# Local attention layers of an eight-stage kernel: entry waits, table timing, a second PSUM bank for the last unit, and stores inside the stage

## The chip, the cores and the metric

The kernel runs on one core of one Trainium2 chip. It is one program of about 102,000 instructions. The metric is the device time of one execution in microseconds (us). The engines are PE (TensorE, matrix multiplies; PEld its weight loads), DVE (VectorE), ACT (ScalarE), POOL (GpSimd) and SP (SyncE, which here only issues DMAs). Each runs its own instruction stream in order, and they meet at semaphores.

## The reference, cut to what matters

Eight blocks in a row work on 8 batches of 256 tokens with 128 channels. Each block's result is normalised and added to the residual. The change touches only the last one, six layers of local attention with a feed-forward part:

```python
x = x + _layernorm(_L3_ffn_ref(_layernorm(x), ...))

for i in range(DEPTH):
    x = attn_layer(shift_tokens(x), Wqkv[i], q_scale[i], k_scale[i], Wo[i]) + x
    x = ffn_layer(shift_tokens(x), ln_g[i], ln_b[i], W1[i], b1[i], W2[i], b2[i]) + x
# attn_layer: q, k, v of 16 heads of 64; l2-normalised; rotated by tables that hold
# cos, sin, a decay and the layer's q_scale / k_scale; softmax over windows of 32 + 32 keys; Wo
# ffn_layer: layernorm, W1, a * gelu(gate), W2
```

## The kernel before, in words

The order of all work is written out by hand. `build` runs the eight stages one after the other. Ahead of a stage `normalise_x` makes `M.xn`, the normalised tokens (16 tiles of 128 tokens, in 4 groups; DVE makes groups 0 and 2 at L495, ACT groups 1 and 3 at L489). Behind it `mark_end` drains the engines, and `add_up` normalises the stage's result `M.y` and adds it to the residual `M.x`: moments, a reciprocal square root by DVE alone (L414 to L425), the scaling (L489, L495), and per group the sum (L519) and the statistics for the next stage (L522). After the last stage SP stores `M.x` in 4 DMAs.

The last stage is `stage_local`. A **unit** is one batch in one layer: 6 x 8 = 48 units, `UNITS`. All engines loop over the same list of **steps** `s`, with `n, p = divmod(s, 8)`: a unit has 8 steps, one for each pair of heads, and a step holds work of several units at once:

- raw rows: PE multiplies a quarter row block of q or k (`a = s + 15` or `s + 16`, L3182), DVE rotates it with the tables (`dve_rope`, L3331 to L3334), POOL adds the halves (L3479, `rope_sum`), ACT squares (L3278), DVE sums the squares (L3438);
- roots of the lengths, twice a unit (`root_of`: DVE L3355, ACT L3259 and L3261, DVE L3361 to L3365);
- POOL scales the rows (L3492, `normed`), PE turns them (L406);
- scores (L3152), softmax, values (L3167), and the output projection `wo` (L3128, in steps `p` 3 and 4 of the next unit);
- two units behind: the feed-forward part (`center`, `moment`, `ones`, `gates`, `third`, `linear`, `out`). Its products, those of v and the projection share one PSUM bank, `room = Bench(M, (1,))`: `fills(s)` says which fill stands in which step, early or late, and each fill waits until the one before it was read.

The rotation tables of a layer are four POOL instructions (L3471). POOL makes them at `a = s + 15`, in the step in which DVE first needs them (`p` is 1 there). The wait in `dve_rope` is on the signal `tables`.

On entry PE turns the four groups of `M.xn` (L406 into banks 0 to 3), and signals `tile_turned`. POOL then zeroes seven places (`cleared`, L3457) and casts two constants. DVE (L3372) and ACT (L3270) copy the turned groups to `X` only once POOL has cleared all places, and PE waits for all copies, all clears and the constants before its first step.

At the end, when the last unit has been fed (L3404, L3405), DVE copies `X` (L3445, L3446), PE turns it back (16 times L406), ACT copies it to `M.y` (L3321), and `add_up` follows.

## Time and profile before

| | us |
|---|---|
| median of 3 runs | 3864.39 (3860.45 to 3868.89) |
| the profiled execution's own time | 3863.01 |
| its span in the profile | 3861.7 |
| PE busy over the span | 3142.8 (81%) |
| DVE, ACT, POOL busy | 2700.2, 2240.3, 1456.3 |
| granted clock of PE, mean | 0.929 of full |

The profile's page gives each engine's busy time, a strip of the span in 40 slices, and the chain of work that ended last. The last stage begins at about 1903 us of the span and takes the rest, half of the kernel. Its slices read 9 (90% busy or more) for PE nearly everywhere. The first of the last stage's boundaries between layers lies in the window from 2181 us, an ordinary unit in that from 3614 us. The views used below are the timeline (each row an instruction or several alike in a row: start, duration, engine, line, output and input, count, and in brackets how long the engine stood idle before it and what ended that), the busy time in chosen windows, and the answer for one source line.

### The profile page before, as it was taken

Reading aid. Unit: us, or ns where it says so; the run is one execution under the profiler, and the core shown is the slowest. Engines: PE = TensorE matmul, PEld = TensorE weight load, DVE = VectorE, ACT = ScalarE, POOL = GpSimd, SP = SyncE. Lnnn points to the kernel's source line nnn. Section 1 sums busy time; section 2 is a strip of 40 time slices with the busy share of each in tenths; the row PEclk is TensorE's granted clock in tenths of the full one; section 3 lists DMA queues with packets and bytes.
Section 4 is the critical chain, followed back from the end, with each engine's and each line's share of the span. In section 5 each row is a group of like instructions: output and inputs, shape, how many; then the busy total and the mean of one; then the engine's idle time right before and its main releaser. Section 6 shows DMA issues by size and latency. Waiting matters only on the chain.

```text
span 3861.7 us, 102257 instructions
## 1 busy us (share of the span) xinstructions
PE 3142.8 (81%) x41309; PEld 2040.7 (53%) x41309; DVE 2700.2 (70%) x7080; ACT 2240.3 (58%) x5612; POOL 1456.3 (38%) x1443
## 2 busy tenths in 40 slices
PE   6877865727776879777589999999999999999996
PEld 4544544612323546445346666666666666666664
DVE  6466666637895554589687777777777777777763
ACT  4234442426653332268557777777777777777773
POOL 0110011336671000000166556566656655656550
PEclk9989987968997989889899999999999999999996
DMA  1000002710000000000001011102010201110110
GB/s 54 1 5 1 1 12 58 221 62 0 1 0 5 2 1 1 30 1 1 30 21 31 22 31 50 31 22 60 22 31 22 60 22 31 50 31 22 31 24 19
DMA packets 50437, 108.05 MB, mean 28 GB/s; under 512 B 7360, under 2 KB 17472, under 8 KB 48176
## 3 DMA queue, kind: packets, MB, share of 16 engines
q1 hardware_dynamic: 47440, 96.33, 9.1%
q0 software_dynamic: 2528, 5.18, 0.7%
q8 instruction: 328, 5.37, 0.6%
q14 instruction: 141, 1.16, 0.1%
HBM read 52.27 MB, written 5.18 MB: 15 GB/s over the span
## 4 chain that ended last, share of the span: by engine, by line
PE 45%; DVE 23%; ACT 13%; issue 5%; POOL 3%; DMA 1%; POOLq 0%; SPq 0%; DVEq 0%; ACTq 0%
PE psum L3182 5%; PE psum L3128 5%; PE psum L401 5%; PE psum L3167 4%; PE psum L406 4%; PE psum L3088 4%; PE psum L1145 4%; PE psum L1998 3%; DVE scratch L3331 3%; PE psum L1199 2%; DVE xnT L3438 2%; DVE xnT L3363 2%; PE psum L3152 1%; DVE scratch L3333 1%; ACT weights L1388 1%
## 5 line engine op out<-in xcount | busy, mean ns | idle before, releaser
L3479 POOL TENSOR_TENSOR scratch<-scratch 128x512 f32<-128x512 f32 x384 | 488.7, 1273 | 434.9 <-DVE scratch L3334 434.9
L406 PEld LDWEIGHTS psum<-table,scratch 128*128 128x128 f32 (+1 forms) x2284 | 283.3, 145 | 297.3 <-issue 237.2
L3182 PE MATMUL psum<-weights,scratch 128*128 128x512 f32 x768 | 418.7, 628 | 18.7 <-ACT y L3278 11.5
L406 PE MATMUL psum<-table,scratch 128*128 128x128 f32 (+1 forms) x2284 | 369.8, 283 | 46.3 <-DVE scratch L2699 11.8
L3492 POOL TENSOR_TENSOR scratch<-scratch,xnT 128x512 f32<-128x512 f32 x384 | 401.6, 1046 | 0.0
L3331 DVE TENSOR_TENSOR scratch<-psum,xnT 128x512 f32<-128x512 f32 x384 | 264.6, 689 | 173.8 <-PE psum L3182 153.6
L3311 ACT COPY scratch<-psum 128x512 f32<-128x512 f32 x384 | 225.7, 588 | 163.8 <-PE psum L406 158.0
L3278 ACT ACTIVATE y<-psum 128x512 f32<-128x512 f32 x384 | 230.8, 601 | 120.6 <-DVE scratch L3334 108.0
L3438 DVE TENSOR_REDUCE xnT<-y 128x8 f32<-128x512 f32 x384 | 254.0, 661 | 1.4
L1145 PE MATMUL psum<-scratch 32*128 32x256 f32 (+1 forms) x2560 | 179.1, 392 | 69.3 <-DVE weights L1406 20.5
L3413 DVE TENSOR_REDUCE scratch<-psum 128x4 f32<-128x256 f32 x384 | 161.4, 420 | 73.8 <-PE psum L3152 72.3
L3088 PE MATMUL psum<-weights,scratch 128*64 128x512 f32 x768 | 207.1, 618 | 1.2 <-ACT scratch L3226 1.2
L3250 ACT ACTIVATE scratch<-psum,scratch 128x64 f32<-128x64 f32 x768 | 178.1, 316 | 46.8 <-DVE scratch L3413 42.7
L3182 PEld LDWEIGHTS psum<-weights,scratch 128*128 128x128 f32 x768 | 136.0, 194 | 126.6 <-issue 78.6
L3485 POOL TENSOR_TENSOR y<-scratch 128x256 f32<-128x256 f32 x192 | 117.9, 614 | 206.3 <-DVE scratch L3421 206.3
L3250 ACT ACTIVATE y<-psum,scratch 128x64 f32<-128x64 f32 x768 | 179.1, 324 | 2.8
L3152 PE MATMUL psum<-scratch 64*32 64x64 f32 x12288 | 175.4, 223 | 0.0
L1145 PEld LDWEIGHTS psum<-scratch 32*128 32x128 f32 x2560 | 119.1, 192 | 106.2 <-DVE weights L1406 32.0
L406 PE MATMUL psum<-table,xn 128*128 128x128 f32 x112 | 25.1, 415 | 183.3 <-DVE xn L495 183.3
L406 PE MATMUL psum<-table,y 128*128 128x128 f32 x784 | 152.5, 279 | 22.6 <-DVE y L495 20.8
L3167 PE MATMUL psum<-xn,scratch 64*64 64x32 f32 x6144 | 129.6, 222 | 47.5 <-ACT scratch L3311 33.0
L3485 POOL TENSOR_TENSOR y<-y,scratch 128x256 f32<-128x256 f32 x192 | 117.9, 614 | 128.0 <-DVE scratch L3421 127.7
(527 smaller groups left out, 7741.3 us busy)
## 6 DMA issues: line engine op xcount, KB each, us to landing
scratch<-scratch SPq DMA_DIRECT2D x96, 256.0 KB, 3.2
scratch<-experts_dram SPq DMA_DIRECT2D x47, 384.0 KB
scratch<-scratch SPq DMA_DIRECT2D x96, 128.0 KB, 3.2
weights<-layer_dram SPq DMA_DIRECT2D x6, 1357.0 KB, 9.5
weights<-layer_dram SPq DMA_DIRECT2D x6, 1356.5 KB, 6.9
scratch<-scratch SPq DMA_DIRECT2D x96, 64.0 KB, 2.9
weights<-gqa_dram SPq DMA_DIRECT2D x2, 1738.5 KB, 8.8
results_dram<-scratch SPq DMA_DIRECT2D x11, 256.0 KB
```

The lines of the kernel that those rows point to most:

```text
L406: return self.nc.tensor.transpose(out, src, self.c("ident")[0:k, 0:k])
L1145: last = mm(bank(n)[:, col:col + size], A.head(rows, n, at, P), A.head(cols, n, by, size), start=not A.causal, stop=True, skip_group_check ...
L3088: last = mm(bank[64 * r:64 * r + 64], window(n)[:, 64 * j:64 * j + 64], weight(n, "wqkv")[:, at:at + 512], start=True, stop=True)
L3167: last = mm(SUMS[64 * h:64 * h + 64, j, QB * q:QB * q + QB], V[u % 2][64 * r:64 * r + 64, 4 * j + q, pair * LDIM:(pair + 1) * LDIM], turne ...
L3182: mm(raw_bank(a), window(m)[:, i * P:i * P + P], weight(m, "wqkv")[:, at:at + 512], start=True, stop=True).then_inc(S("rows_made").up(), 1)
L3250: last = nc.scalar.activation(E[s % 2][:, 2 * j + (h ^ j), :], scores(s)[:, h, 64 * j:64 * j + 64], ACT.Exp, bias=small[s % 4][:, 0, 2 * h ...
L3278: nc.scalar.activation(sq[a % 2], raw_bank(a), ACT.Square).then_inc(S("squared").up(), 1)
L3331: tt(heads(out), src, bc(cosine, LDIM), ALU.mult).then_inc(dve.link(), 1)
L3438: red(lengths[m % 2][:, 0, 2 + 8 * q:10 + 8 * q], heads(sq[a % 2]), AX, ALU.add).then_inc(S("lens").up(), 1)
L3479: gtt(out, out, sines, ALU.add).then_inc(S("rope_sum").up(), 1)
L3485: gtt(probs[t % 2], E[t % 2], over_keys(small[t % 4][:, 1, :]), ALU.mult).then_inc(S("divided_pool").up(), 1)
L3492: gtt(out, out, lengths[m % 2][:, 1, 2 + 8 * q:10 + 8 * q].unsqueeze(2).broadcast_to([P, HB, LDIM]), ALU.mult).then_inc(S("normed").up(), 1)
```

## The change: what it does

1. **Entry.** PE turns `M.xn` into banks 4 to 7. DVE and ACT copy without waiting for `cleared`. POOL begins once DVE has made its tiles of `M.xn`, clears one column of `X`, makes the tables of layer 0, and then clears the rest and casts. PE starts its steps at once: a unit of the first layer waits for its own columns, scores wait for the clears. ACT loads its table behind its copies.
2. **Tables.** `pool_rope(l)` makes a layer's tables at `s + 22`, seven steps sooner (in a step with `p` 2, where before it was `p` 1). DVE's wait stands.
3. **Last unit.** Unit 47 uses bank 0 for all its fills but v (`last_room`), and its steps are moved ahead by 2 (`AHEAD`; its projection by 1, all 8 pairs in one step). `unit_at` says so for each kind of work.
4. **Stores.** The last layer's batches are finished in five sets (2, 2, 2, 1 and 1 batches; `SETS`), each in the 8 steps that begin 24 steps behind its last unit's first: PE turns them back from `X` in two halves with a wait between, ACT copies, DVE takes statistics and variances; the root rides in `root_of`; ACT scales, DVE adds to `M.x`, SP stores. `mark_end` and `add_up` are not called for this stage.

```diff
-    room = Bench(M, (1,))
+    room, last_room = Bench(M, (1,)), Bench(M, (0,))
+    AHEAD = 2
+    def unit_at(s, lag, p, ahead=AHEAD):
+        last = UNITS - 1
+        if s == 8 * (last + lag) + p - ahead:
+            return last
+        n, q = divmod(s - p, 8)
+        return n - lag if q == 0 and 0 <= n - lag < last else None
+    SETS = [(UNITS - 8, 2), (UNITS - 6, 2), (UNITS - 4, 2), (UNITS - 2, 1), (UNITS - 1, 1)]
+    set_at = {f + k - 1 + 3: e for e, (f, k) in enumerate(SETS)}
...
+        if p == 0 and n in set_at:
+            early.append(("set", set_at[n], "y_out", set_at[n]))
...
         elif key == "project":
-            pe_project(n, range(4))
+            pe_project(n, range(8 if n == UNITS - 1 else 4))
...
+        elif key == "set":
+            pe.wait_ge(S("fed"), 2 * tiles_of(n)[-1][0] + 1)
+            for i, (f, j) in enumerate(tiles_of(n)):
+                last = nc.tensor.transpose(bank[:, i * P:i * P + 64], low(f)[:, j * P:j * P + P], c("ident")[0:64, 0:64])
+            last.then_inc(pe.link(), 1)
+            pe.settle()
+            for i, (f, j) in enumerate(tiles_of(n)):
+                last = nc.tensor.transpose(bank[:, i * P + 64:i * P + P], high(f)[:, j * P:j * P + P], c("ident")[64:P, 64:P])
+            last.then_inc(S("y_turned").up(), 1)
...
     def pe_program():
         M.wait_loaded(pe, "layer0")
-        pe_turn(M, M.xn)
-        pe.wait_ge(S("lowest"), GROUPS - 1)
-        pe.wait_ge(S("highest"), GROUPS - 1)
-        pe.wait_ge(S("cleared"), CLEARS - 1)
-        pe.wait_ge(S("tables"), 0)
+        for g in range(GROUPS):
+            wait_xn(M, pe, g)
+            for k in range(4):
+                last = M.flip(M.bank(4 + g)[:, P * k:P * k + P], M.xn[:, 4 * g + k, :])
+            last.then_inc(S("tile_turned").up(), 1)
...
-        dve.wait_ge(S("tables"), m // BATCH + 1)
+        dve.wait_ge(S("tables"), m // BATCH)
...
     def act_program():
...
+            if p == 5 and n in set_at:
...
+                act.wait_ge(S("y_scaled"), e)
+                for i in range(k):
+                    last = nc.scalar.activation(done[e % 2][:, i, :], done[e % 2][:, i, :], ACT.Identity, bias=r[:, 1, i:i + 1],
+                                                scale=lengths[(n + 1) % 2][:, 1, 66 + i:67 + i])
...
+    SET_WORK = {1: dve_see_set, 2: dve_set_variance, 4: dve_set_shift, 6: dve_set_add}
...
     def dve_program():
         M.wait_loaded(dve, "layer0")
-        dve.wait_ge(S("cleared"), CLEARS - 1)
...
     def pool_program():
-        M.wait_loaded(pool, "layer0")
-        pool.wait_ge(S("tile_turned"), GROUPS - 1)
...
+        pool.wait_ge(S("xn_dve"), 2 * GROUPS - 1)
+        nc.gpsimd.memset(X[64:P, :, 0:1], 0.0).then_inc(S("cleared").up(), 1)
+        pool.wait_ge(S("cleared"), 0)
+        pool_rope(0)
...
-            a = s + 15
-            if 0 <= a < PARTS and a % (8 * BATCH) == 0:
...
+            l, k = divmod(s + 22, 8 * BATCH)
+            if k == 0 and 0 < l < DEPTH:
+                pool_rope(l)
...
     def sp_program():
...
+        for e, (f, k) in enumerate(SETS):
+            tiles = slice(2 * (f % BATCH), 2 * (f % BATCH) + 2 * k)
+            sp.wait_ge(S("x_sum"), e)
+            nc.sync.dma_start(M.out[:, tiles, :], M.x[:, tiles, :]).then_inc(M.out_sem, 16)
```

`dve_see_set` takes one statistics instruction per tile, `dve_set_variance` six small instructions with two waits among them, `dve_set_shift` one, `dve_set_add` one sum over all tiles of the set.

The instruction order on POOL at the stage's entry. L3457 are the clears, L3459 and L3460 the casts, L3471 the tables, L3479 the first sums. Before:

```order
L3457 MEMSET scratch 64x8
L3457 MEMSET scratch 128x8x32 x2
L3457 MEMSET scratch 32x512 x4
L3459 CAST scratch<-table 128x128
L3460 CAST scratch<-table 128x128
L3471 TENSOR_TENSOR xnT<-table,weights 128x128 x4
L3479 TENSOR_TENSOR scratch<-scratch 128x512 x10
```

Now (L3546 and L3552 are the clears, L3540 the tables, L3566 the sums):

```order
L3546 MEMSET scratch 64x8
L3540 TENSOR_TENSOR xnT<-table,weights 128x128 x4
L3552 MEMSET scratch 128x8x32 x2
L3552 MEMSET scratch 32x512 x4
L3554 CAST scratch<-table 128x128
L3555 CAST scratch<-table 128x128
```

The tables went from behind the clears and casts to behind the first clear.

On POOL at a layer's boundary, now, the tables (L3540) stand between the row scaling of step `p` 1 (L3579) and the sum of step `p` 2 (L3566); L3572 divides the probabilities:

```order
L3566 TENSOR_TENSOR scratch<-scratch 128x512
L3572 TENSOR_TENSOR y<-scratch 128x256
L3579 TENSOR_TENSOR scratch<-scratch,xnT 128x512
L3540 TENSOR_TENSOR xnT<-table,weights 128x128 x4
L3566 TENSOR_TENSOR scratch<-scratch 128x512
L3572 TENSOR_TENSOR y<-y,scratch 128x256
```

Before, the same four stood seven rounds of these three later, ahead of the sum of the step in which the new layer's first rows are rotated.

On PE at the end of the program. L3167 are the values of the last pair of heads, L3114 and L3115 `third`, L3118 `linear`, L3128 the projection, L401 `out`, L3095 `center`, L3099 `moment`, L3104 `ones`, L3110 `gates`. Before:

```order
L3167 MATMUL psum<-xn,scratch 64x32 x16
L3114 MATMUL psum<-weights 85x256
L3115 MATMUL psum<-weights 85x256
L3118 MATMUL psum<-weights 128x256 x2
L3128 MATMUL psum<-xnT,weights 128x256 x2
L3128 MATMUL psum<-xn,weights 128x256 x6
L401 MATMUL psum<-weights 128x256 x3
L3095 MATMUL psum<-scratch,table 128x256
L3099 MATMUL psum<-table,stats 128x1 x2
L3104 MATMUL psum<-weights,table 128x128 x2
L3110 MATMUL psum<-weights 128x256 x2
```

Now (L3204 values, L3140 and L3141 `third`, L3164 projection, L3144 `linear`, L3121 `center`, L3125 `moment`, L3130 `ones`, L3136 `gates`, L3150 and L3154 the two halves of a set):

```order
L3204 MATMUL psum<-xn,scratch 64x32 x16
L3140 MATMUL psum<-weights 85x256
L3141 MATMUL psum<-weights 85x256
L3164 MATMUL psum<-xnT,weights 128x256 x2
L3164 MATMUL psum<-xn,weights 128x256 x6
L3144 MATMUL psum<-weights 128x256 x2
L3121 MATMUL psum<-scratch,table 128x256
L3125 MATMUL psum<-table,stats 128x1 x2
L401 MATMUL psum<-weights 128x256 x3
L3130 MATMUL psum<-weights,table 128x128 x2
L3136 MATMUL psum<-weights 128x256 x2
L3150 MATMUL psum<-table,scratch 128x64 x2
```

The last unit's projection went ahead of the unit before's `linear`, its `center` and `moment` ahead of that unit's `out`, and a set stands behind its `gates`. The 16 turns at the end are gone.

## Rows read from the trace of the kernel before

**Rows 1.** Windows: length, busy PE, PEld, DVE, ACT, POOL, granted clock, DMA.

```profile
2181.00:2223.90 42.90, 38.72 (x653) 26.04 (x652) 30.18 (x76) 28.84 (x82) 24.48 (x29) 0.92 0.10 24
3614.00:3652.20 38.20, 35.96 (x653) 24.35 (x653) 30.07 (x76) 28.83 (x80) 23.03 (x24) 1.00 0.12 26
```

**Rows 2.** Timeline of the stage's entry (start, duration, engine, line, what, count, idle before).

```profile
1903.45 3.19 ACT L489 ACTIVATE xn<-x,stats 128x128 f32<-128x128 f32 x8 [5.99 <-DVE stats L484]
1903.45 2.14 DVE L495 TENSOR_SCALAR xn<-x,stats 128x128 f32<-128x128 f32 x8
1904.71 3.65 PE L406 MATMUL psum<-table,xn 128*128 128x128 f32 x16 [16.62 <-DVE xn L495]
1908.50 3.15 POOL L3457 MEMSET scratch<- 64x8 f32 x7 [294.27 <-PE psum L406]
1911.74 2.48 DVE L3372 COPY scratch<-psum 64x512 f32<-64x512 f32 x4 [6.15 <-POOL scratch L3457]
1912.21 1.51 POOL L3471 TENSOR_TENSOR xnT<-table,weights 128x128 f32<-128x128 f32 x4
1915.16 5.62 PE L3182 MATMUL psum<-weights,scratch 128*128 128x512 f32 x8 [6.81 <-ACT scratch L3270]
1917.24 0.69 DVE L3331 TENSOR_TENSOR scratch<-psum,xnT 128x512 f32<-128x512 f32 x1 [3.03 <-PE psum L3182]
```

**Rows 3.** Timeline at the first and the last of five layer boundaries.

```profile
2180.21 0.66 DVE L3438 TENSOR_REDUCE xnT<-y 128x8 f32<-128x512 f32 x1
2181.95 1.51 POOL L3471 TENSOR_TENSOR xnT<-table,weights 128x128 f32<-128x128 f32 x4
2183.55 0.69 DVE L3331 TENSOR_TENSOR scratch<-psum,xnT 128x512 f32<-128x512 f32 x1 [2.68 <-issue]
...
3421.00 1.51 POOL L3471 TENSOR_TENSOR xnT<-table,weights 128x128 f32<-128x128 f32 x4
```

**Rows 4.** The answer for line L3331: its idle time over the whole span.

```profile
  issue: 13.4, 5
```

**Rows 5.** Timeline of an ordinary unit, DVE and POOL.

```profile
3650.76 1.27 POOL L3479 TENSOR_TENSOR scratch<-scratch 128x512 f32<-128x512 f32 x1 [1.35 <-DVE scratch L3334]
3650.82 1.27 DVE L3363 SCALAR_TENSOR_TENSOR xnT<-xnT 128x34 f32<-128x34 f32 x1
3655.05 0.42 DVE L3391 TENSOR_TENSOR weights<-stats,psum 128x256 f32<-128x256 f32 x1
3658.28 0.69 DVE L3331 TENSOR_TENSOR scratch<-psum,xnT 128x512 f32<-128x512 f32 x1 [1.10 <-PE psum L3182]
3659.71 1.27 POOL L3479 TENSOR_TENSOR scratch<-scratch 128x512 f32<-128x512 f32 x1 [1.41 <-DVE scratch L3334]
3664.88 1.27 POOL L3479 TENSOR_TENSOR scratch<-scratch 128x512 f32<-128x512 f32 x1 [2.33 <-DVE scratch L3334]
3693.23 0.42 DVE L3391 TENSOR_TENSOR weights<-stats,psum 128x256 f32<-128x256 f32 x1
```

**Rows 6.** Timeline of the tail, from the last values to the last statistics.

```profile
3802.59 1.08 PE L3167 MATMUL psum<-xn,scratch 64*64 64x32 f32 x32 [0.52 <-DVE xn L3383]
3806.67 2.07 PE L3118 MATMUL psum<-weights 128*128 128x256 f32 x4 [1.07 <-DVE weights L3425]
3809.71 2.08 PE L3128 MATMUL psum<-xnT,weights 128*128 128x256 f32 x4 [0.97 <-DVE weights L3396]
3824.93 0.42 DVE L3391 TENSOR_TENSOR weights<-stats,psum 128x256 f32<-128x256 f32 x1 [2.11 <-PE psum L3104]
3838.71 0.49 DVE L3405 SCALAR_TENSOR_TENSOR scratch<-psum,weights,scratch 64x256 f32<-64x256 f32 x1
3850.26 0.17 DVE L451 SCALAR_TENSOR_TENSOR stats<-stats 128x16 f32<-128x16 f32 x1
3853.06 4.73 ACT L489 ACTIVATE y<-y,stats 128x128 f32<-128x128 f32 x12 [6.93 <-DVE stats L484]
3859.36 0.87 DVE L522 BATCH_NORM_STATS2 stats<-x 128x6 f32<-128x128 f32 x4
```

More of the change, by code:

```diff
@@ L3042, in room_of, with tiles_of, room_for @@
+    def tiles_of(e):
+        f, k = SETS[e]
+        return [(f + i // 2, i % 2) for i in range(2 * k)]
+    def room_for(key, n):
+        return last_room if n == UNITS - 1 and key[0] != "v" else room
     def room_of(key, n):
-        return room.bank((key, n))
+        return room_for(key, n).bank((key, n))
     def fills(s):
         n, p = divmod(s, 8)
-        unit = lambda k: 0 <= k < UNITS
         early, late = [], []
-        if p == 0 and unit(n - 2):
-            late.append(("ones", n - 2, "scaled", n - 2))
@@ L3065, in fills @@
-        if p >= 6 and unit(n + 1):
+        if p == 0 and n in set_at:
+            early.append(("set", set_at[n], "y_out", set_at[n]))
+        for key, lag, at, when, signal, step in (
+                ("ones", 2, 0, late, "scaled", lambda f: f), ("gates", 2, 1, early, "gelu", lambda f: 3 * f + 1),
+                ("third", 2, 2, early, "gated", lambda f: 3 * f), ("linear", 2, 2, late, "gated", lambda f: 3 * f + 2),
+                ("project", 1, 3, early, "added", lambda f: 2 * f + 1), ("out", 2, 4, late, "fed", lambda f: 2 * f + 1),
+                ("center", 1, 5, early, "centered", lambda f: f), ("moment", 1, 5, late, "var_out", lambda f: f)):
+            f = unit_at(s, lag, at, 1 if key == "project" else AHEAD)
+            if f is not None:
+                when.append((key, f, signal, step(f)))
@@ L3350, in dve_clamp @@
         x = lengths[m % 2][:, 0, first:last]
+        if last > 66:
+            dve.settle()
         if m < UNITS:
```

183 lines of the change are left out of this document (107 added, 76 removed).

## The prediction

> **What bounds the kernel now.** I read the busy windows first, then the timeline at the four places that the change touches. In an ordinary unit PE is busy 35.96 of 38.20 us at the full clock, DVE 30.07, ACT 28.83 and POOL 23.03 [rows 1]. So PE sets the pace, with small gaps, and DVE and ACT have a fifth to a quarter left. The same instruction of two neighbouring units (L3391) starts at 3655.05 and 3693.23, 38.18 us apart [rows 5]: that is the rhythm of nearly all 48 units. Anything that moves the total must break this rhythm at a few places, shorten the entry or the tail, or change the rhythm itself. PE is 0.92 clocked in the boundary unit and 1.00 in the other [rows 1], which says that something stalls it there.
>
> **Entry.** PE's 16 turns end at 1904.71 + 3.65 = 1908.36. Only then does POOL clear for 3.15 us, then DVE copies, ACT copies, and the first raw rows start at 1915.16; DVE's first rotation is at 1917.24, 2.08 behind them [rows 2]. In the changed order PE goes on to the raw rows at once. Their columns are there: ACT's rows of `M.xn` end at 1903.45 + 3.19 = 1906.64 and DVE's at 1905.59 [rows 2], and group 0 can be copied by about 1907.3, while PE still turns the last group. Raw rows then start at 1908.4 instead of 1915.16: **6.8 us** sooner. What could be late next is POOL. It starts at 1905.6; 3.15 of clears, 1.51 of tables and about 0.6 of casts (estimated from the clears' size) end near 1911.0. DVE's first rotation, at 1908.4 + 2.08 = 1910.5, needs only the first clear and the tables (about 1907.4), and its sum on POOL is wanted at about 1911.9. So POOL's work is covered with 0.9 us to spare; without cover it costs at most that much again. Bounds 5.8 to 7.2.
>
> **Tables.** At a boundary DVE is done with its step at 2180.21 + 0.66 = 2180.87, PE's rows are ready, and DVE stands until POOL has made the tables (2181.95, 1.51 us): 2.68 us [rows 3]. It happens 5 times, 13.4 us in all [rows 4]. But the loss is larger. The tables of the first and the last boundary start at 2181.95 and 3421.00 [rows 3], 1239.05 us for 4 layers, that is 32 units; 32 x 38.18 = 1221.76. The rest is 17.29, or 4.32 for each boundary. The other 1.6 us is the clock: the boundary unit has 0.92 granted, so PE runs a stretch of it at the lower of its two levels (1.2 against 2.4 GHz) behind the stall, and in the ordinary unit, without a stall, it never does [rows 1]. I take it that without the stall the clock does not fall: 5 x 4.32 = 21.6. The new place costs POOL 1.51 us once a layer, in step `p` 2, where POOL stands idle for 1.41 us anyway (the gap before the sum at 3659.71) [rows 5]. That leaves about 0.1 to 0.2 us of delay, 0.5 for all five. Net **21.1 us**; bounds 12.2 (only the wait goes, each new place costs 0.24) and 21.6. The Trainium skill, page "TensorE: Matmul & The Clock Gate", Part 1, says the same of the mechanism: the lower clock is the default, idling brings it back, activity releases it. By that rule the whole 21.6 goes with the stall; by the wait alone it would be 13.4.
>
> **Sets inside the full program.** Sets 0 and 1 stand in units 44 and 46. Each adds: on PE 8 narrow turns and a wait for its own queue. 16 full turns took 3.65 at half clock, 0.23 each [rows 2]; narrow ones at full clock are at most half of that, 0.9 for 8, with the wait about 1.3. On ACT a copy (0.6) and 4 scalings of 4.73 / 12 = 0.39 [rows 6], 2.2 in all. On DVE 4 statistics (0.87 [rows 6]), six small ones and a longer clamp at 0.17 each [rows 6] with waits, about 1.1, a shift and a sum of 0.7: 2.8. What of it is on the path: PE's 1.3 fully, since PE leads there. DVE's statistics lie in step 1, ahead of a gap of 1.10 us [rows 5]: nothing. The small ones come in step 2, where the next rotation follows without a gap: 1.1. ACT's 1.6 of scalings in step 5 delay the next square, partly covered: 1.1. Together 3.5 for set 0. Set 1 is in a unit without raw rows and rotations, so only about 2.2. Sum **+5.7 us**; bounds 2.6 (PE alone, twice) and 12.6 (nothing covered: 1.3 + 2.2 + 2.8 = 6.3, twice).
>
> **One rule speaks against this part.** DVE's L3363 starts at 3650.82, 0.06 behind POOL's sum at 3650.76, and takes 1.27 us, just as long as POOL's; a DVE instruction as small took 0.17 with POOL idle [rows 5, 6]. So a small DVE instruction can wait out a whole POOL one. The new variances are such. They come at the end of step 2, though, and there POOL stands idle for 2.33 us until DVE's next rotation [rows 5], so I charge no such wait. The Trainium skill, page "SBUF — State Buffer", section "SBUF: two separate sides", describes this as an exclusive lock on a port pair that DVE and POOL share, taken by DVE instructions with two SBUF inputs. By the rule taken alone each of three waiting groups would cost a POOL instruction, some 3.5 us more a set.
>
> **Last unit.** Before, one bank forces the order third, `linear`, projection. The last values end at 3802.59 + 1.08 = 3803.67 and the last unit's L3391 starts at 3824.93 [rows 6], 21.3 us later. In it PE stands 1.07 before `linear` and 0.97 before the projection [rows 6], each time for DVE's gating, and unit 46's `out` and sum (2.5) stand ahead of the last unit's `center`. Now the projection follows `third` directly, and `out` runs while the last unit's variance goes through its root. Saved: 1.07 + 0.97 and about 1.9 of the 2.5, 3.9. Against it: set 2 (8 turns at the half clock and a copy) sits in front, +1.2. Net **2.7 us**; bounds 0 and 4.5. PE's clock decides most of that width, since it changes level here.
>
> **End.** Before, the last feed ends at 3838.71 + 0.49 = 3839.20 and the last sum at about 3859.3, where its statistics start (3859.36) [rows 6]: 20.1 us of copy, turns, moments over 16 tiles, 12 scalings, four sums. Now two tiles are left. From the feed: rest of set 3 on DVE and ACT, which covers the four turns, 1.7; copy 0.4; 2 statistics 0.43; seven small DVE steps at 0.2 (0.17 [rows 6] and a wait) 1.4; two on ACT 0.5; root 0.6; shift 0.2; two scalings 0.8; sum 0.4. That is 6.4, so 13.7 less. Set 3's turns delay `third` of the last unit by about 0.3. Net **13.4 us**; bounds 12 and 15. The stores of sets 0 to 3 lie beside other work. The last store, half as large as before, is counted as before.
>
> **Sum.** -6.8 - 21.1 + 5.7 - 2.7 - 13.4 = -38.3 us. The profiled execution took 3863.0 of its own; 3824.7 by this. The median of the runs is 1.4 above it, which gives 3826; I say 3825.
>
> **Rivals.**
> 1. The clock falls at the boundaries all the same. For it: a unit has many small gaps, and the sets add more. Against it: no ordinary unit shows it [rows 1]. Gain 38.3 - (21.1 - 12.2) = 29.4: about 3835. Chance 0.08.
> 2. The sets cost their full engine time, 12.6, and their stalls bring a stretch at the lower clock each (1.6, twice): 15.8 in place of 5.7, gain 28: about 3836. For it: L3363's 1.27 us beside POOL [rows 5], and that three engines are hit in one unit. Against it: the gaps in [rows 5]. Chance 0.14.
> 3. Sets almost free (2.6) and the tail at the full clock: gain 43: about 3821. Chance 0.08.
> 4. Slower. L3363 waits for POOL twice a unit because the two start together [rows 5]. Tables and entry shift POOL against DVE; if the rhythm settled where one more small DVE instruction a unit waits 1.27 us, 45 units would cost 57 and the time would be about 3882. It decides from 38.3 / 45 = 0.85 us a unit. Against it: after each boundary, disturbed by over 4 us, the rhythm was 38.18 again (the 1239.05 leaves no room for anything else). Chance 0.02; a smaller shift of the rhythm that eats all the gain, 0.02.
>
> My forecast, about 3825, has 0.66. Its own range is 3819 to 3831; with rivals 1 to 3 taken in as far as 2 in 10 allow, 3818 to 3836. A difference of 0.2% is 7.7 us, about what a measurement of this kernel can tell from none. All cases but the fourth are far past it: faster 0.96, same 0.02, slower 0.02.
>
> **What the profile after would show.** Entry: first raw rows within 0.2 of the last turn, POOL idle before its first sum. Boundaries: no wait on DVE at the layer's first rotation, 8 units at 305.4 us, clock 1.00 throughout. Sets: unit 44 at about 41.7 instead of 38.2. Tail: last sum 6.4 behind the last feed. I am wrong if the distance between two layers' tables stays near 309.7, if units 44 and 46 grow by over 6 us, or if an ordinary unit no longer takes 38.18.

## The result: 1.3% faster, and below the range

| | before | changed |
|---|---|---|
| median of the runs timed together, us | 3863.77 (4 runs, 3860.45 to 3868.89) | 3812.48 (4 runs, 3810.68 to 3813.61) |
| the profiled execution's own time, us | 3863.01 | 3813.27 |
| span of the profiled execution, us | 3861.7 | 3812.0 |
| granted clock of PE, mean | 0.929 | 0.935 |

The ratio is 0.9866, with a 95% interval from 0.9853 to 0.988; timed again later it was 0.9876 (0.986 to 0.9893; 3813.03 against 3860.66 us). The change saves 51.3 us by the medians, and the interval keeps well clear of 1. The forecast was 38.3 us, 3825 us with a range down to 3818, so the time came out 12.5 us below the forecast. Each of the five terms has the sign that was forecast, but four of them lie outside the bounds that the prediction gave them. No rival had this outcome: the third came nearest, with 3821.

To see where it went I cut both traces at the same instructions and took differences of starts. The table also holds a second profile of the changed kernel and three experiments told below. Its first line says where the last stage begins; what stands ahead of that is the work of unchanged code. "Scores" are cut where DVE takes the largest score of a step (L3413 before), and "scaling" is DVE's product with the inverse deviation (L3391 before).

| us, from start to start | before | changed | changed, again | no set 2 | old ending | improved, again |
|---|---|---|---|---|---|---|
| last L495 of the kernel begins at | 1903.45 | 1901.70 | 1904.57 | 1897.50 | 1902.06 | 1905.33 |
| to the first rotation | 13.79 | 6.20 | 6.18 | 6.10 | 6.15 | 6.20 |
| to the first scores | 42.49 | 42.45 | 42.47 | 42.46 | 42.45 | 42.44 |
| unit 0 of scores | 32.57 | 32.01 | 32.05 | 32.09 | 32.09 | 32.01 |
| units 1 to 46 | 1770.56 | 1750.19 | 1750.82 | 1750.77 | 1749.77 | 1750.82 |
| last unit's first to last scores | 29.24 | 28.60 | 27.41 | 27.41 | 28.91 | 27.40 |
| to the last values | 10.49 | 11.37 | 11.49 | 10.64 | 10.46 | 10.46 |
| to the last unit's scaling | 22.34 | 16.83 | 16.09 | 16.36 | 12.79 | 14.09 |
| to the last feed | 13.78 | 13.77 | 13.77 | 13.77 | 13.77 | 12.10 |
| to the end of the span | 22.99 | 8.88 | 8.55 | 9.60 | 22.95 | 7.95 |
| the last stage in all | 1958.25 | 1910.30 | 1908.83 | 1909.20 | 1919.34 | 1903.47 |

The seven unchanged stages ahead vary. In the 14 profiles of this study the last stage began anywhere from 1897.50 to 1909.36 us, and two executions of one program began it at 1901.70 and 1904.57. Of the 49.7 us between the two profiled executions, 1.75 is theirs and no part of the change. So single runs are compared below by "the last stage in all".

**The windows of a boundary unit, an ordinary unit and the unit with set 0, changed kernel** (they answer to [rows 1]):

```profile
2169.30:2207.50 38.20, 36.01 (x653) 24.44 (x653) 30.07 (x77) 28.81 (x81) 23.01 (x24) 1.00 0.12 27
2207.50:2245.70 38.20, 35.97 (x653) 24.37 (x654) 30.08 (x77) 28.82 (x81) 23.00 (x24) 1.00 0.12 26
3619.70:3659.50 39.80, 36.77 (x661) 24.93 (x660) 33.02 (x89) 30.57 (x86) 23.47 (x24) 1.00 0.12 26
```

The boundary unit reads like any other: the same 653 PE records, the same 38.2 us, the clock at 1.00. Unit 44 has 8 records more and is 1.6 us longer.

**The stage's entry in the changed kernel's timeline** (answers to [rows 2]):

```profile
1902.96 3.64 PE L406 MATMUL psum<-table,xn 128*128 128x128 f32 x16 [16.62 <-DVE xn L495]
1904.15 1.47 DVE L3460 COPY scratch<-psum 64x512 f32<-64x512 f32 x2 [0.32 <-PE psum L406]
1904.17 1.51 POOL L3540 TENSOR_TENSOR xnT<-table,weights 128x128 f32<-128x128 f32 x4
1905.61 2.98 POOL L3552 MEMSET scratch<- 128x256 f32 x6
1906.40 3.17 PE L3221 MATMUL psum<-weights,scratch 128*128 128x512 f32 x6
1907.90 0.69 DVE L3376 TENSOR_TENSOR scratch<-psum,xnT 128x512 f32<-128x512 f32 x1 [0.57 <-PE psum L3221]
1908.89 0.29 POOL L3555 CAST scratch<-table 128x128 bf16<-128x128 f32 x1
1909.33 1.26 POOL L3566 TENSOR_TENSOR scratch<-scratch 128x512 f32<-128x512 f32 x1
```

The raw rows start at 1906.40, 0.20 before the turns' recorded end, and the first rotation follows in 1.50, not 2.08 us. The granted clock was 0.50 during the turns in both kernels. Before, PE then stood for 6.81 us, and the clock was 0.50 again from the first raw row to the first rotation (1915.16 to 1917.20). Now it rises during the first rows and is 0.86 over 1906.40 to 1909.60. POOL's second cast ends at 1909.18 and DVE's rotation at 1909.24; POOL's sum starts at 1909.33.

**POOL in the step with the tables, and DVE at the new layer's first rotation** (answers to [rows 3, 4]):

```profile
2136.18 1.04 POOL L3579 TENSOR_TENSOR scratch<-scratch,xnT 128x512 f32<-128x512 f32 x1
2137.18 1.51 POOL L3540 TENSOR_TENSOR xnT<-table,weights 128x128 f32<-128x128 f32 x4
2138.65 1.28 POOL L3566 TENSOR_TENSOR scratch<-scratch 128x512 f32<-128x512 f32 x1
...
2173.61 0.66 DVE L3526 TENSOR_REDUCE xnT<-y 128x8 f32<-128x512 f32 x1
2175.37 0.69 DVE L3376 TENSOR_TENSOR scratch<-psum,xnT 128x512 f32<-128x512 f32 x1 [1.10 <-PE psum L3221]
```

The four fill POOL's gap and the sum follows without idle time. DVE's wait of 2.68 us is gone; the 1.10 that is left is the wait for PE of every such step [rows 5].

**The tail, from the last values on** (answers to [rows 6]):

```profile
3772.52 1.08 PE L3204 MATMUL psum<-xn,scratch 64*64 64x32 f32 x32 [0.52 <-DVE xn L3471]
3775.32 1.91 PE L3164 MATMUL psum<-xnT,weights 128*128 128x256 f32 x4
3777.03 3.12 PE L3164 MATMUL psum<-xn,weights 128*128 128x256 f32 x12
3784.44 0.20 ACT L3301 ACTIVATE xnT<-xnT 128x2 f32<-128x2 f32 x1
3785.66 0.48 DVE L3492 SCALAR_TENSOR_TENSOR scratch<-psum,weights,scratch 64x256 f32<-64x256 f32 x1 [1.49 <-PE psum L401]
3786.69 0.16 DVE L3411 TENSOR_TENSOR xnT<-xnT 128x2 f32<-128x2 f32 x1
3789.35 0.42 DVE L3479 TENSOR_TENSOR weights<-stats,psum 128x256 f32<-128x256 f32 x1 [1.50 <-PE psum L3130]
3803.12 0.49 DVE L3493 SCALAR_TENSOR_TENSOR scratch<-psum,weights,scratch 64x256 f32<-64x256 f32 x1
3804.43 0.88 ACT L3364 ACTIVATE table<-table,xnT 128x128 f32<-128x128 f32 x2 [2.96 <-DVE xnT L3446]
3805.21 0.35 ACT L3272 COPY table<-psum 128x256 f32<-128x256 f32 x1
3809.37 0.43 DVE L3452 TENSOR_TENSOR x<-x,table 128x256 f32<-128x256 f32 x1 [0.95 <-ACT table L3364]
```

PE goes from the values through `third` into the projection without a wait. Two things here were left to gain: ACT has the last unit's root ready at 3784.64, but DVE takes it up (L3411) at 3786.69, behind the two feeds of unit 46; and ACT's copy of set 4 stands behind set 3's scalings. The last sum ends at 3809.80, 6.19 us behind the last feed's end at 3803.61.

### The profile page after: what moved, and what is told of

Its sections match the earlier page's. It is cut to its first block, busy times and chain, and to the rows that moved or that the text cites. A ratio compares the mean times of both kernels' runs of the same rounds, so it can differ in the third digit from the quotient of the medians.

```text
span 3812.0 us, 102302 instructions
## 1 busy us (share of the span) xinstructions
PE 3127.3 (82%) x41325; PEld 2030.5 (53%) x41325; DVE 2696.3 (71%) x7087; ACT 2240.9 (59%) x5623; POOL 1455.2 (38%) x1443
## 4 chain that ended last, share of the span: by engine, by line
PE 45%; DVE 23%; ACT 14%; issue 5%; POOL 3%; DMA 1%; POOLq 0%; SPq 0%; DVEq 0%; ACTq 0%
PE psum L3164 5%; PE psum L3221 5%; PE psum L401 5%; PE psum L3204 4%; PE psum L3114 4%; PE psum L406 4%; PE psum L1145 4%; PE psum L1998 3%; DVE scratch L3376 2%; PE psum L1199 2%; DVE xnT L3526 2%; DVE xnT L3413 2%; POOL scratch L2609 1%; ACT L3280 1%; PE psum L3189 1%
## 5 line engine op out<-in xcount | busy, mean ns | idle before, releaser
L3566 POOL TENSOR_TENSOR scratch<-scratch 128x512 f32<-128x512 f32 x384 | 488.1, 1271 | 409.9 <-DVE scratch L3379 409.7
L3221 PE MATMUL psum<-weights,scratch 128*128 128x512 f32 x768 | 413.2, 620 | 14.5 <-ACT y L3316 14.1
L3579 POOL TENSOR_TENSOR scratch<-scratch,xnT 128x512 f32<-128x512 f32 x384 | 401.4, 1045 | 0.0
L3114 PE MATMUL psum<-weights,scratch 128*64 128x512 f32 x768 | 207.1, 618 | 1.5 <-ACT scratch L3261 1.5
L3572 POOL TENSOR_TENSOR y<-scratch 128x256 f32<-128x256 f32 x192 | 117.6, 612 | 206.8 <-DVE scratch L3509 206.8
L3204 PE MATMUL psum<-xn,scratch 64*64 64x32 f32 x6144 | 129.5, 223 | 50.0 <-ACT scratch L3350 35.6
L3572 POOL TENSOR_TENSOR y<-y,scratch 128x256 f32<-128x256 f32 x192 | 118.2, 616 | 126.8 <-DVE scratch L3509 126.8
```

Of the source, the lines that this page charges most:

```text
L3114: last = mm(bank[64 * r:64 * r + 64], window(n)[:, 64 * j:64 * j + 64], weight(n, "wqkv")[:, at:at + 512], start=True, stop=True)
L3204: last = mm(SUMS[64 * h:64 * h + 64, j, QB * q:QB * q + QB], V[u % 2][64 * r:64 * r + 64, 4 * j + q, pair * LDIM:(pair + 1) * LDIM], turne ...
L3221: mm(raw_bank(a), window(m)[:, i * P:i * P + P], weight(m, "wqkv")[:, at:at + 512], start=True, stop=True).then_inc(S("rows_made").up(), 1)
L3566: gtt(out, out, sines, ALU.add).then_inc(S("rope_sum").up(), 1)
L3572: gtt(probs[t % 2], E[t % 2], over_keys(small[t % 4][:, 1, :]), ALU.mult).then_inc(S("divided_pool").up(), 1)
L3579: gtt(out, out, lengths[m % 2][:, 1, 2 + 8 * q:10 + 8 * q].unsqueeze(2).broadcast_to([P, HB, LDIM]), ALU.mult).then_inc(S("normed").up(), 1)
```

## The experiments

Each is an edit of the changed kernel. Diffs show only what differs from it. Each ran once, beside the kernel before, which took 3865.2 or 3864.8 us there, but for the last three, which were timed in rounds. A single time is therefore set against the changed kernel's 3812.48 only for orientation; the argument goes by stretches of the profiles.

### Tables: the wait and the clock

First the tables alone were put back:

```diff
-            l, k = divmod(s + 22, 8 * BATCH)
+            l, k = divmod(s + 15, 8 * BATCH)
```

> The changed kernel, with a layer's tables made again in the step in which DVE first needs them. Theory A (the stall costs its wait and a stretch of PE at the lower clock): each of five boundary units grows by 3.9 to 4.8 us over 38.17, 22 us in all, about 3834, and the windows show PE below full clock behind each boundary. Rival B (only the 2.7 us wait counts, the rest came from elsewhere in the change): 2.7 per boundary, 13.4 in all, about 3826.

Then the stall was kept and PE was given something to do in it, 18 products that nobody reads:

```diff
+    FILLER = 18
...
+            if p == 1 and (s + 15) % (8 * BATCH) == 0 and 0 < s + 15 < PARTS:
+                pe.wait_ge(S("exped"), s - 1)
+                for i in range(FILLER):
+                    mm(M.bank(3)[:, 256:384], c("ones"), c("ident"), start=True, stop=True)
             for key, f, _, _ in early:
                 pe_fill(key, f)
```

> As tables_back, and PE works through 18 extra small products (128x128, results unused) while it would stand idle at the five boundaries, so that it never idles long. Theory A (the part over the wait is PE's clock): the granted clock stays at full level, each boundary unit grows by only about 2.8 to 3.2 us, 14 to 16 us in all, about 3827. Rival B (the part over the wait is queueing of DVE, ACT and POOL behind the stall, whatever the clock): boundary units grow by 4 to 5 us as without the extra products, 22 us or more, about 3834.

Eighteen were too many: PE came to `gates` 1.1 us late because of them. So the same again with `FILLER = 12`:

> As tables_back_filled, but with 12 extra small products at each of the five boundaries instead of 18, because the 18 ran 1.1 us past the end of DVE's wait and held up the gates by as much. Theory A (the part over the wait is PE's clock): with the clock full and nothing held up, each boundary unit is 2.7 to 3.0 us over 38.17, 14 us in all over the changed kernel. Rival B (the part over the wait is queueing behind the stall): still 3.7 or more at each.

| | time | five boundary units | each over 38.17 | clock behind the boundary |
|---|---|---|---|---|
| changed | 3812.48 | 38.16 to 38.18 | 0 | 1.00 |
| tables back | 3836.44 | 41.84 to 42.86 | 3.7 to 4.7 | 0.83 in three, 0.66 in two (over 10 us) |
| tables back, 18 products | 3832.48 | 41.84 to 41.86 | 3.7 | 1.00 |
| tables back, 12 products | 3828.00 | 40.81 to 40.82 | 2.65 | 1.00 |

**PE with the tables back**, timeline of the first boundary:

```profile
2174.82 0.67 PE L3204 MATMUL psum<-y,scratch 64*64 64x32 f32 x32
2178.43 1.27 PE L3136 MATMUL psum<-weights 128*128 128x256 f32 x4 [2.94 <-ACT weights L3320]
2179.48 1.91 PE L3221 MATMUL psum<-weights,scratch 128*128 128x512 f32 x2
2181.19 1.06 PE L406 MATMUL psum<-table,scratch 128*128 128x128 f32 x4
```

**and with the 12 products** (24 records, L3213):

```profile
2174.75 0.67 PE L3206 MATMUL psum<-y,scratch 64*64 64x32 f32 x32
2175.35 2.94 PE L3213 MATMUL psum<-table 128*128 128x128 f32 x24
2178.37 1.10 PE L3136 MATMUL psum<-weights 128*128 128x256 f32 x4
2179.31 1.02 PE L3227 MATMUL psum<-weights,scratch 128*128 128x512 f32 x2
2180.16 0.60 PE L406 MATMUL psum<-table,scratch 128*128 128x128 f32 x4
```

In both DVE waits 2.68 us for the tables and `gates` starts at 2178.4. What differs is whether PE was idle for 2.94 us ahead of it. Where it was, the raw rows take 1.91 us and the turns 1.06; where it was busy, 1.02 and 0.60. So the split of the prediction is shown: a boundary cost 2.65 us of wait and, on top, 1.0 to 2.1 us of lower clock. With the tables back the two boundaries with 0.66 are those that grow by 4.7 us. The kernel before had boundary units of 42.93, 42.29, 42.03, 42.69 and 42.93 us; over the changed kernel's 38.17 that is 22.0 us, and all of it is gone. The run with the tables back came out 2.4 us above what was expected of it; its last stage began 2.3 us later than the changed kernel's. By the Trainium skill, page "TensorE: Matmul & The Clock Gate", Part 1, idling brings the lower clock and activity releases it; these two runs agree, with 1.91 against 1.02 us for the same two records.

### Entry

```diff
     def pe_program():
...
+        pe.wait_ge(S("lowest"), GROUPS - 1)
+        pe.wait_ge(S("highest"), GROUPS - 1)
+        pe.wait_ge(S("cleared"), CLEARS - 1)
...
     def dve_program():
...
+        dve.wait_ge(S("cleared"), CLEARS - 2)
...
     def act_program():
...
+        act.wait_ge(S("cleared"), CLEARS - 2)
...
     def pool_program():
...
-        pool.wait_ge(S("xn_dve"), 2 * GROUPS - 1)
+        pool.wait_ge(S("tile_turned"), GROUPS - 1)
```

and `pool_rope(0)` again behind the clears, ACT's table load again ahead of its copies.

> The changed kernel with the entry of before: POOL clears, casts and makes the tables behind the last turn, DVE and ACT copy behind the clears, PE waits for all. Theory: from the start of the stage's normalisation to DVE's first rotation 13.8 us instead of 6.2, and the first two units 0.6 slower from clock, so 7.6 to 8.2 us more, about 3820.5. Rival (part of the gain at the entry is taken back in the first units because DVE and POOL set their pace anyway): less than 6 us more.

It took 3825.05 us, its last stage 1921.7 us, 11.4 over the changed kernel's 1910.3. The first rotation is 13.80 behind L495 again (6.20 in the changed kernel), which is 7.6, and unit 0 takes 33.42 instead of 32.01, 1.4. Of this 1.4 only 0.6 is in the kernel before (32.57); the other 0.85 is this run's own, with the clock at 0.90 in the unit where the kernel before has 0.95. The rest was not the entry's: unit 44, the one with set 0, took 41.51 instead of 39.82, and the windows there show the clock at 0.83 from 3643 to 3653. That is a second price for a set, 3.3 us where PE loses its level in it and 1.65 where it doesn't. PE's longest wait ahead of the fall is this one:

```profile
3643.80 0.67 PE L3207 MATMUL psum<-y,scratch 64*64 64x32 f32 x32 [1.29 <-DVE y L3477]
```

The changed kernel has the same wait at the same place and keeps the upper level:

```profile
3633.88 0.67 PE L3204 MATMUL psum<-y,scratch 64*64 64x32 f32 x32 [1.30 <-DVE y L3471]
```

So the wait alone does not decide whether the clock falls. What else it takes stays open.

### Last unit

Everything of it back (one bank, no moves), and then only the second bank away with the moved steps kept:

```diff
-    AHEAD = 2
+    AHEAD = 0
...
     def room_for(key, n):
-        return last_room if n == UNITS - 1 and key[0] != "v" else room
+        return room
...
-            pe_project(n, range(8 if n == UNITS - 1 else 4))
+            pe_project(n, range(4))
...
```

> The changed kernel with the last unit in the one bank and in its old steps (also its projection in two halves). Theory: 5.5 us more between the last values and the last unit's multiplication by its inverse deviation, less what set 2 then hides, so 4.5 to 6 us, about 3818. Rival (the move is worth only the two waits of PE, 1.07 and 0.97): 2 to 2.5 us, about 3815.

> The changed kernel with all steps of the last unit where it has them, but its fills in bank 1 again, so only the second bank is undone. Theory (the bank is what frees the projection, the center and the moment from the unit before): the projection must wait until the unit before has gated its third part, its linear until the projection was added, about 1.5 to 3 us more between the last values and the last unit's scaling (16.8 us now). Rival (the order alone does it): under 0.5 us more.

| | time | last stage | values to scaling | scaling to last feed |
|---|---|---|---|---|
| changed | 3812.48 | 1910.3 | 16.83 | 13.77 |
| all of it back | 3820.20 | 1916.7 | 23.99 | 13.78 |
| one bank only | 3816.98 | 1916.5 | 22.05 | 15.25 |

With the steps moved, the second bank carries nearly all of the gain: with one bank the tail loses 5.2 + 1.5 = 6.7 us, with all of it back 7.2. Both are more than was expected of them (1.5 to 3, and 4.5 to 6). The forecast had 3.9 for both together. What the second bank would be worth with the steps left in their old places was not tried.

### End and sets

The sets away and the old ending back (DVE's copies of `X`, PE's 16 turns, ACT's copies, the drain, the sums of all tiles):

```diff
-    set_at = {f + k - 1 + 3: e for e, (f, k) in enumerate(SETS)}
+    set_at = {}
...
+        for g in range(GROUPS):
+            for k in range(4):
+                last = M.flip(M.bank(2 + g)[:, P * k:P * k + P], M.xnT[:, GROUP * g + P * k:GROUP * g + P * k + P])
...
-            if name == "layer0":
-                return
             M.mark_end()
```

> The changed kernel without sets: after the last unit all of it is copied, turned, normalised and stored at once as before. Theory: units 44 and 46 back at 38.2 and 34.3 and the step with set 2 0.9 shorter, so 3.1 us less ahead of the last feed, and 20.1 instead of 6.2 us from the last feed to the last sum: 10.8 us more in all, about 3824. Rival (the sets cost more than the units show, by memory traffic or PE's clock later on): 8 us more or less.

It took 3822.71, its last stage 1919.3 us, 9.0 more than the changed kernel's where 10.8 was expected. The end costs 22.95 us from the last feed instead of 8.88: 14.1. Unit 44 is back at 38.18, so set 0 cost 1.65 in the changed kernel. Unit 46 was expected at 34.3 without set 1 and took 35.37, with the clock at 0.95 in it; with set 1 it is 34.88, at 1.00. But in the tail something larger showed: from the last values to the scaling it took 12.79 us, 4.0 less than with the sets. I read that as the cost of set 2, which stands there, by way of the clock. The next run took only set 2 away. It stores batches 4 and 5 without the last stage's result, so it leaves out work and serves as a probe only:

```diff
-    SETS = [(UNITS - 8, 2), (UNITS - 6, 2), (UNITS - 4, 2), (UNITS - 2, 1), (UNITS - 1, 1)]
+    SETS = [(UNITS - 8, 2), (UNITS - 6, 2), (UNITS - 2, 1), (UNITS - 1, 1)]
...
+        nc.sync.dma_start(M.out[:, 8:12, :], M.x[:, 8:12, :]).then_inc(M.out_sem, 16)
```

> Set 2 (batches 4 and 5) is left out of the changed kernel: PE doesn't turn it, nobody copies, scales or adds it, and these two batches are stored without the last layers' result. All else stands as in the changed kernel. The stretch from the last scores to the last unit's scaling took 28.2 us in the changed kernel and 23.25 in the one without any set. Theory A (set 2's cost in the tail is mainly the clock: its turns and the wait for its own queue come where PE already waits for DVE, and PE then stays at the lower level for 20 us): the clock in that stretch stays at its upper level, and the stretch takes 23.3 to 24.0; the time falls by 4.2 to 5, to about 3808. Rival B (it is set 2's own work on PE, DVE and ACT, and the clock is low there anyway because the last unit leaves PE little to do): PE shows the lower level in this stretch as before, and the stretch takes 25.5 to 26.5, gain 1.7 to 2.7, about 3810.5. Rival C (sets 0, 1 and 3 are the cause): the stretch stays above 27.

It took 3807.97 us, which would fit the first theory, but its stages ahead happened to be 4.2 us shorter; its last stage took 1909.2. The stretch from the last scores to the scaling took 27.00 us (10.64 + 16.36), against 28.20 and 27.58 in the two profiles of the changed kernel. So set 2 costs 0.6 to 1.2 us, no more than two executions of one program differ by, and my first theory, with 23.3 to 24.0, falls. Theories B (25.5 to 26.5) and C (above 27) are not told apart. The windows from the last values to the scaling show where the 4 us appear (length, then the columns of [rows 1]). The kernel before:

```profile
3802.60:3825.00 22.40, 15.12 (x72) 10.50 (x72) 4.04 (x13) 3.89 (x9) 0.00 (x0) 0.65 0.00 1
```

The changed kernel, first profile:

```profile
3772.50:3789.40 16.90, 12.85 (x72) 9.48 (x72) 5.96 (x25) 5.72 (x15) 0.00 (x0) 0.70 0.04 10
```

Its second profile:

```profile
3775.00:3791.10 16.10, 12.10 (x72) 9.11 (x72) 5.92 (x25) 5.72 (x15) 0.00 (x0) 0.82 0.00 1
```

Without set 2:

```profile
3767.00:3783.40 16.40, 12.95 (x72) 9.75 (x72) 4.05 (x13) 3.88 (x9) 0.00 (x0) 0.71 0.00 0
```

With the old ending:

```profile
3771.90:3784.70 12.80, 9.39 (x72) 7.19 (x72) 4.00 (x13) 3.89 (x9) 0.00 (x0) 1.00 0.00 1
```

PE has the same 72 records in each, which take 9.39 us at a clock of 1.00 and 12.95 at 0.71. The old ending's run had the upper level in all of this stretch. It had paid a part ahead of it, where its clock was lower for a while. Against the changed kernel's second profile it gains 3.3 us here, and had lost 1.5 in the last unit's scores (28.91 against 27.41) and 0.5 in unit 46 (35.37 against 34.91). I take the rest for luck of where its low stretch fell; with one profile of this kernel that isn't shown. The changed kernel itself had 0.70 in one execution and 0.82 in the next, with 16.83 and 16.09 us; from the last unit's first scores to its scaling that makes 56.80 and 54.99, so chance alone moves this stretch by 1.8 us. That it would be 1.00 in every execution without sets 0, 1 and 3 was not tried.

### Two waits on DVE in the tail

In the tail DVE computes a set's variance behind its wait for the gating, and the last unit waits for the root in which it rides. The first edit puts the variance ahead of that wait:

```diff
-    SET_WORK = {1: dve_see_set, 2: dve_set_variance, 4: dve_set_shift, 6: dve_set_add}
+    SET_WORK = {1: dve_see_set, 4: dve_set_shift, 6: dve_set_add}
...
+            if n in set_at and p == 2:
+                dve_set_variance(set_at[n], n)
             f, k = unit_at(s, 2, 2), GLU_PARTS[2][1]
```

> The changed kernel with a set's six small variance instructions ahead of DVE's wait for the third gelu (1.46 us idle there) instead of at the end of the step. Theory (a set costs what of its work no gap covers, here 0.8 us of these six): the unit of set 0 takes 39.0 instead of 39.8, that of set 1 about 0.2 less, in all 1 us less. Rival (the set's cost is PE's turns and ACT's scalings): no difference.

3809.34 us, last stage 1906.6, 3.7 below the changed kernel's first profile and 2.3 below its second. To the values it takes 10.48 (0.9 and 1.0 less), to the scaling 14.86 (2.0 and 1.2 less); the clock in that last stretch is 0.84, against 0.70 and 0.82. Unit 44 gained 0.36, not 0.8, and unit 46 nothing. So the expectation (1 us, in the units) was wrong as to the place: the gain lies in the tail. It rests on one profile, and some of it may be the clock's.

The second edit adds two moves to it: unit 46's `out` and feeds stand behind the last unit's `ones` and scaling, and the last feed behind set 3's scalings:

```diff
+    def fed_at(s):
+        if s == 8 * (UNITS + 1) + 5:
+            return UNITS - 1
+        if s == 8 * UNITS + 7:
+            return UNITS - 2
+        f = unit_at(s, 2, 5)
+        return f if f is not None and f < UNITS - 2 else None
...
+            if key == "out":
+                f = out_at(s, 0)
...
-            f = unit_at(s, 2, 5)
+            f = fed_at(s)
```

(`out_at` moves unit 46's `out` to step 8 * UNITS + 6 in the same way.)

> Three moves of order on top of the changed kernel, all in the tail but one: a set's variance stands ahead of DVE's wait for gelu in step 2 (as in the run before, 3.1 us); unit 46's output product and its two feeds stand behind the last unit's `ones` and its scaling, so that DVE has not to feed unit 46 before it can prepare the last unit's root; the last feed comes two steps later in the list, so that set 3's root, shift and scalings stand ahead of it. Theory A (in the tail the order on DVE sets the time): the variance gives 3 us, and of the 2.05 us that the last unit's root lay ready on ACT before DVE took it up, 1.5 to 2 come back in the stretch from the last values to the last unit's scaling; at the end ACT's copy of set 4 no longer stands behind set 3's 0.88 us of scalings, 0.4 us. 3807 in all, ratio to the kernel before about 0.985. Rival B (PE's low clock sets the tail): the moved work meets PE at half clock and only changes place; no more than the variance's 3 us, 3809.

The median of its 4 runs is 3814.46 (3804.31 to 3815.18), ratio 0.9862 (0.9846 to 0.9878): no different from the changed kernel's, and neither the 3807 nor the 3809 that was expected. Its last stage took 1903.7 us, 6.6 less, but it began at 1909.36, 7.7 later. So it was timed once more, with the changed kernel on the same chip.

> The changed kernel as it is, beside its three moves (the other run of this call, on the same chip). Theory: the stretch from the last stage's first L495 to the end takes 1910.3 us, as in its first profile, whatever the seven stages ahead take; these vary by several us from execution to execution (1897.5 to 1909.4 in the profiles so far) and make the spread of the times, 3810 to 3814.

> The same three moves as in the last but one run, with no edit, timed beside the changed kernel. Its profile then had a last stage 6.6 us shorter (1903.7 against 1910.3) and a total no shorter, since the seven stages ahead took 7.7 longer. Theory A: that was chance of this execution or chip; the last stage takes 1903.7 to 1905 again and the time comes out 5 to 7 us below the changed kernel's on this chip, about 3806. Rival B: the text of the program, changed in the last stage, shifts the stages ahead and eats it every time; the stages ahead take 1907 to 1910 again, against 1900 to 1902 in the other run, and both times are equal.

| timed together, medians of 4 | time | ratio to before | last stage begins | last stage |
|---|---|---|---|---|
| changed | 3813.03 (3811.49 to 3814.78) | 0.9876 (0.986 to 0.9893) | 1904.57 | 1908.8 |
| with the three moves | 3810.18 (3808.30 to 3813.95) | 0.9872 (0.9855 to 0.9888) | 1905.33 | 1903.5 |

The changed kernel's last stage was expected at 1910.3 again and took 1.5 us less; the last unit's scores (clock 0.93, then 1.00) and the stretch to the scaling account for it.

**The kernel with the three moves, second profile**: PE's `ones` of the last unit (L3150) stands ahead of unit 46's `out` (L401), and DVE's scaling (L3499) ahead of its feeds (L3512).

```profile
3787.51 1.20 PE L3150 MATMUL psum<-weights,table 128*128 128x128 f32 x4 [3.14 <-ACT weights L3359]
3788.50 2.77 PE L401 MATMUL psum<-weights 128*128 128x256 f32 x6
3788.75 0.42 DVE L3499 TENSOR_TENSOR weights<-stats,psum 128x256 f32<-128x256 f32 x1 [1.24 <-PE psum L3150]
3791.31 0.48 DVE L3512 SCALAR_TENSOR_TENSOR scratch<-psum,weights,scratch 64x256 f32<-64x256 f32 x1 [2.14 <-PE psum L401]
```

In the last stage the three moves save 5.4 to 6.6 us in both pairs of profiles, of which the variance is 2.3 to 3.7. They also cost something: unit 46 takes 35.9 us in both, 1.0 more than in the changed kernel, and its clock is 0.95 instead of 1.00. Unit 46 in the changed kernel's second profile, and with the three moves:

```profile
3701.20:3736.10 34.90, 30.25 (x627) 21.57 (x627) 19.18 (x59) 25.89 (x77) 13.45 (x16) 1.00 0.13 29
3700.90:3736.80 35.90, 31.52 (x625) 22.47 (x627) 20.22 (x58) 25.87 (x77) 13.43 (x16) 0.95 0.12 28
```

In the time of the whole kernel the saving isn't settled: the medians differ by 2.85 us, the intervals of the ratios overlap almost wholly, and the stages ahead, which the edit doesn't touch, take several us more or less. Theory A expected 5 to 7 us of time. Rival B expected the last stage to begin at 1907 to 1910 with the moves and at 1900 to 1902 without; it began at 1905.33 and 1904.57, which speaks against a fixed shift by the changed program text. The 7.7 us of the first pair were then most likely chance, or the chip's, since the two runs of that pair were not made together.

## Why the prediction was right in kind and short in size

**Entry: 6.8 forecast, 8.2 measured** (7.6 to the first rotation, 0.6 in unit 0). The step that failed is "DVE's first rotation, at 1908.4 + 2.08": the 2.08 us between rows and rotation was taken from rows in which PE ran low after its 6.8 us of waiting. Without the wait it is 1.50, and the rows start 0.25 us sooner than forecast besides. POOL was covered, but by 0.06 us and not by 0.9: its second cast ends at 1909.18, and the rotation that its sum waits for ends at 1909.24.

**Tables: 21.1 forecast, 22.0 measured.** The steps held, the one on the clock too. The 0.5 us charged for the new place was nothing: POOL's gap of 1.41 took in the 1.51 and the next unit has 38.16.

**Sets 0 and 1: +5.7 forecast, +2.3 measured** (39.82 for 38.17 and 34.88 for 34.27). This is the largest miss, the step "What of it is on the path: PE's 1.3 fully", with 1.1 for DVE's small ones and 1.1 for ACT. Four narrow turns took 0.46 us, so 0.98 for both halves with the 0.06 between them, and PE had idled 0.41 near there. Step by step, unit 44 is behind its neighbours by 0.41 and 0.09 us in steps 0 and 1, where the turns stand, by 0.74 in step 2, where the six small instructions and the longer clamp take 0.81 (not 1.1), and by 0.34 in step 6, behind ACT's scalings. Moving the six elsewhere gave back 0.36 of the 0.74, so this division is in part a reading. For set 1 it is weaker still: no run leaves out set 1 alone, and without any set unit 46 took 35.37. The argument against the waits behind POOL held for the variances:

```profile
3631.25 0.15 DVE L3433 TENSOR_TENSOR xnT<-xnT 128x4 f32<-128x4 f32 x1
3631.86 0.16 DVE L3440 SCALAR_TENSOR_TENSOR xnT<-xnT 128x4 f32<-128x4 f32 x1
3632.06 0.18 DVE L3405 TENSOR_SCALAR xnT<-xnT 128x36 f32<-128x36 f32 x1
```

They stand where POOL is idle (from 3630.50 to 3633.58), and each took 0.15 to 0.18 us. The lock between DVE and POOL that the Trainium skill describes (page "SBUF — State Buffer", section "SBUF: two separate sides") holds DVE back only while POOL works, so with POOL idle it asks for no wait here, and the trace agrees. The prediction's 3.5 us by that rule had left this out; the sum did not use them.

**Last unit: 2.7 net forecast, 4.6 measured** (5.51 less to the scaling, 0.88 more to the values). The step that failed is "Saved: 1.07 + 0.97 and about 1.9": going back costs 7.2, not 3.9. The two waits were read rightly, but what PE executed between was priced as if it kept its level. PE's 72 records took 15.12 us before and 12.85 after. That is 2.3 us of clock, and the prediction had said that the clock decides most of the width here, without putting it in the sum. Set 2 was +1.2 in the forecast and 0.6 to 1.2 in the run without it. A further 0.6 us (29.24 against 28.60) lies in the last unit's own scores, was in no term, and varies with the clock as well: 27.41 in the second profile.

**End: 13.4 forecast, 14.1 measured.** From the last feed to the last sum it took 6.19 for the 6.4 that was added up, and set 3 delayed the last unit by nothing instead of 0.3.

**Not in the forecast at all:** 1.75 us of the stages ahead, which is chance, and 0.015 us in each of some 40 ordinary units (38.18 against 38.165), 0.6 us, which is chance too: the changed kernel's second profile has 38.18. Sum of the misses: 1.4 + 0.9 + 3.4 + 1.9 + 0.6 + 0.7 + 1.75 + 0.6 = 11.3 of the 11.4 us by which the profiled executions differ from the forecast. The median before is 0.8 above its profiled execution and the one after 0.8 below, which makes 51.3 of the 49.7.

The range failed because the bounds of the terms were too tight, and not because the terms were joined wrongly. With every term at its favourable bound the gain is 7.2 + 21.6 - 2.6 + 4.5 + 15 = 45.7 us, which is 3818, the lower end of the range. Measured were 8.2, 22.0, -2.3 and 4.6: four of five beyond their bounds, the end alone inside with 14.1. For entry and last unit the reason is the same. Where PE stops waiting it also ran faster, and the terms priced only the wait. For the sets it is the gaps next to the added work. The stages ahead gave 1.75 us more by luck, but the last stage alone, 48.0 us shorter, was beyond the range too.

## What to carry to other kernels

A PE stall is to be priced with the clock behind it: here 2.65 us of wait came with 1.0 to 2.1 us more, and the PE records after the entry's wait of 6.81 us ran at the lower level, so that their durations were no measure of the time without the wait. Work added next to short idle gaps is to be priced less the gap: here 5.7 us were charged for two sets and 2.3 came. The bound of a term must hold what the clock can do to the instructions around a wait; the wait's own length is no bound. Single profiles of this kernel are best compared by the stage that was changed.

## What the runs showed of the hardware that I had not expected

- Idle PE for 2.94 us costs more than the idle time: the next raw rows took 1.91 us for 1.02, and the turns 1.06 for 0.60. Twelve products without any use, in the same stall, removed that cost and saved 7.6 us in the five boundary units (the whole times are 3836.44 and 3828.00).
- One and the same set of instructions cost 1.65 us in unit 44 where the clock stayed at 1.00, and 3.3 where it was 0.83 over 10 us. PE's longest wait there was 1.30 us in the first case and 1.29 in the second.
- With two moves of order in the tail, unit 46 had about as many PE records as before (625 for 627) and a clock of 0.95 instead of 1.00, in both profiles, and took 1.0 us longer.
- One program, executed twice, had 0.70 and 0.82 as the mean clock over the same 72 PE records in the tail, and the same stretch took 16.83 and 16.09 us. The Trainium skill, page "TensorE: Matmul & The Clock Gate", Part 1, says of a kernel's start that the number of its slow products differs from run to run; this is the like of it in the middle of a program.
- Seven stages of unchanged code took from 1897.5 to 1909.4 us in 14 profiles. The spread arises in the first stage (260.9 to 264.0 us from its start to the second's), the fourth (222.5 to 227.9) and the fifth and sixth together (788.1 to 793.2); the others agree within 0.6 us.
